# Four conditional layers in one kernel: group 0's tables beside stage 0, and the order of three pieces of work

## The reference

```
x = x + einsum('bct,bcd->bdt', x, W0[cond[b]])                 # L0: one of 16 64x64 matrices per sample
x = x + (causal_conv(x, K1) + D1 * x) * (t < len1[b])          # L1: state space kernel K1[h, 1024]
x = x + x @ W2.T + bias + scale[a] * (x @ A[a].T) @ B[a].T     # L2: over time, 1024x1024, adapter a of 8, rank 16
u = x * (t < len3[b]);  x = x + (causal_conv(u, K3) + D3 * u) * (t < len3[b])   # L3
K[h, l] = 2 Re sum_n C'[h, n] exp(dtA[h, n] * l)
```

## Time and profile before

| | us |
|---|---|
| median of 3 runs | 1615.21 (1614.43 to 1619.71) |
| the profiled execution | 1616.8, of which its span 1615.0 |
| PE busy | 1508.3 (93%) |
| DVE busy | 1251.3 (77%) |
| ACT busy | 746.6 (46%) |
| POOL busy | 573.4 (36%) |

### The profile page before, as it was taken

How to read it: one execution, slowest core, us unless ns; L and a number is a source line. 1 busy time by engine, 2 the same in 40 slices (tenths; PEclk the granted TensorE clock), 3 DMA queues, 4 the chain that set the end, 5 groups by cost and what they waited for, 6 DMA issues and landing times.

```text
span 1615.0 us, 36864 instructions
## 1 busy us (share of the span) xinstructions
PE 1508.3 (93%) x14983; PEld 1303.5 (81%) x14983; DVE 1251.3 (77%) x1525; ACT 746.6 (46%) x1083; POOL 573.4 (36%) x260
## 2 busy tenths in 40 slices
PE   7777776889999999999999999999999999999998
PEld 6677774678878787878887878788888888888887
DVE  6888876879596969697878787887878686969663
ACT  3445343435453535454545454545444454545443
POOL 2111104473333333333333434343434343434030
PEclk9898888999999999999999999999999999999999
DMA  7799995567666675757585748484848484858532
GB/s 222 254 346 380 333 373 196 126 128 186 134 170 155 155 169 137 187 126 183 128 193 118 199 113 211 99 222 90 220 97 217 90 225 100 222 103 209 110 131 67
DMA packets 455239, 287.63 MB, mean 178 GB/s; under 512 B 331512, under 2 KB 410880, under 8 KB 453056
## 3 DMA queue, kind: packets, MB, share of 16 engines
q1 hardware_dynamic: 405888, 174.57, 46.5%
q10 hardware_dynamic: 49216, 110.98, 20.2%
HBM read 161.30 MB, written 75.96 MB: 147 GB/s over the span
## 4 chain that ended last, share of the span: by engine, by line
PE 77%; DVE 11%; DMA 6%; issue 4%; ACT 2%; DVEq 0%; ACTq 0%; SPq 0%
PE ps L861 35%; PE ps L945 8%; PE ps L770 7%; PE ps L814 6%; PE ps L841 5%; DMA arena<-in_x_dram 5%; PE ps L870 5%; PE ps L958 4%; PE ps L718 3%; PE ps L780 2%; DVE arena L1790 2%; DVE gbuf L1744 1%; PE ps L654 1%; ACT arena L1297 1%; DVE arena L1635 1%
## 5 line engine op out<-in xcount | busy, mean ns | idle before, releaser
L861 PE MATMUL ps<-arena,w2t 128*128 128x256 f16 x4608 | 521.5, 273 | 0.0
L861 PEld LDWEIGHTS ps<-arena,w2t 128*128 128x128 f16 x4608 | 450.7, 98 | 55.8 <-DVE arena L1836 0.2
L588 POOL TENSOR_TENSOR arena<-arena 128x1024 f32<-128x1024 f32 x32 | 80.0, 2501 | 818.0 <-DVE arena L1797 402.6
L1840 DVE TENSOR_TENSOR arena<-arena 128x512 f16<-128x512 f32 x128 | 106.4, 831 | 125.6 <-ACT arena L1286 125.6
L1286 ACT ACTIVATE arena<-arena 128x512 f16<-128x512 f32 x128 | 80.6, 630 | 240.4 <-DVE arena L1836 239.4
L718 PE MATMUL ps<-arena 128*128 128x128 f32 x1024 | 143.3, 303 | 49.5 <-DVE arena L1635 28.2
L718 PEld LDWEIGHTS ps<-arena 128*128 128x128 f32 x1024 | 135.3, 215 | 55.1 <-DVE arena L1635 31.4
L814 PE MATMUL ps<-arena 128*128 128x512 f16 (+1 forms) x768 | 138.5, 331 | 24.2 <-DVE gbuf L1744 15.8
L1273 ACT ACTIVATE arena<-ps,biasx 128x256 f32<-128x256 f32 x256 | 105.0, 468 | 108.6 <-PE ps L861 56.9
L814 PEld LDWEIGHTS ps<-arena 128*128 128x128 f16 x768 | 72.4, 99 | 83.0 <-DVE gbuf L1744 24.2
L945 PE MATMUL ps<-arena 128*128 128x256 f16 (+1 forms) x1536 | 137.0, 246 | 0.0
(11 more groups left out here) (239 smaller groups left out, 2666.5 us busy)
## 6 DMA issues: line engine op xcount, KB each, us to landing
w2t<-w_scratch ACTq DMA_DIRECT2D x96, 512.0 KB, 4.0
arena<-in_x_dram SPq DMA_DIRECT2D x64, 512.0 KB, 8.0
out_dram<-arena SPq DMA_DIRECT2D x64, 512.0 KB, 3.4
gbuf<-x_scratch SPq DMA_DIRECT2D x120, 256.0 KB, 4.3
arena<-krow_scratch SPq DMA_DIRECT2D x32, 512.0 KB, 8.9
gbuf<-w_scratch ACTq DMA_DIRECT2D x32, 512.0 KB, 3.7
x_scratch<-arena ACTq DMA_DIRECT2D x14, 1024.0 KB, 9.4
x_scratch<-arena ACTq DMA_DIRECT2D x14, 896.0 KB, 7.6
```

Source lines behind the costliest of these rows:

```text
L861: mm = nc.tensor.matmul(ps[:, bank, n * HW:(n + 1) * HW], weight(p, n, part, k), xx[:, :, k, :], start=(fresh and n == 0 and k == 0 and q ...
L1840: tt(x3_quarter(x3l, h0, row), x3part[slot].rearrange("p (k h b) -> p k h b", k=2, h=2), x3_quarter(x3h, h0, row), ALU.subtract).then_inc( ...
```

## The change

Four edits. (1) The first row of ids has a semaphore of its own, VectorE casts it alone first, and the other two behind the one-hot and the diagonal. (2) Group 0's small tables and kernel rows are loaded ahead of the last quarter of stage 0, into weight space that is free by then; GpSimd makes group 0's u and v of L1 as soon as the last tables of buffer 0 are stored, into other tiles (`table_home`, `base_home` and `tab_home` name the new tiles for the first tables and the old ones else); ScalarE and VectorE split the bases ahead of their last copy of stage 0, one of the two last `keep_x1` copies goes to ScalarE, and `turn_g1` and `table_lo` move ahead. ScalarE's first load of a streamed weight slot also waits for g1's reversal and the finished tables, the third for the split bases. (3) In group 0 the two resident block products come ahead of the low-rank products (the 24 matmuls of L841, now `low_products()`) and wait for two x2 heads only. (4) In every body with a following group, VectorE's two past sums come two places later, behind conv rows 1 and 2.

```diff
+        v32_first = part_of(gbuf, 16, 6).rearrange("p (h n t) -> p h n t", h=HG, n=3)
+        m32_first = part_of(gbuf, 32, 4).rearrange("p (h t) -> p h t", h=HG)
+        u32_first = part_of(gbuf, 36, 4).rearrange("p (h t) -> p h t", h=HG)
+        tab_first = w2t[:, 0, 3].rearrange("p s k o -> p (s k o)").bitcast(F32)[:, 0:TAB]
+        g1n_first = w2t[:, 1:3, 3].rearrange("p q s k o -> p q (s k o)").rearrange("p q (m t) -> p q m t", t=CHUNK)
...
+        def is_first(v, g):
+            return v == 0 and isinstance(g, int) and g == 0
...
         @block.sync
-                sp.dma_start(ids[:, n, :], row.rearrange("(o b) -> o b", o=1).to_broadcast([P, B])).then_inc(ids_loaded, 16)
+                sp.dma_start(ids[:, n, :], row.rearrange("(o b) -> o b", o=1).to_broadcast([P, B])).then_inc(ids_loaded if n else ids0_loaded, 16)
             def load_g(v, g):
+                if is_first(v, g):
+                    src = bass.AP(krow_t, 0, [[1, P], [4 * KROW, 2], [KROW, 4], [1, CHUNK]])
+                    for q in range(2):
+                        sp.dma_start(to[:, q], src[:, q]).then_inc(g1_loaded, 8 * 2)
...
-            stage0(0, True)
-            with sp.Fori(1, NBLK // 2) as i:
-                stage0(i, False)
...
-            sp.wait_ge(x1_stored[0][NPART - 1], 16 * NBLK // 2)
+            stage0(0, True)
+            with sp.Fori(1, NBLK // 2 - 1) as i:
+                stage0(i, False)
             sp.wait_ge(tab_stored[0], 16)
+            sp.wait_ge(w2_turned, LOT_W + 3 * 3)
             for n in range(2):
                 load_tab(0, 0, n)
-            sp.wait_ge(s0_summed, NBLK * STEPS)
             sp.wait_ge(krow_stored, 16 + 32)
             load_g(0, 0)
+            stage0(NBLK // 2 - 1, False)
+            sp.wait_ge(x1_stored[0][NPART - 1], 16 * NBLK // 2)
             wait_u(0, 0)
             turn_u(0, 0)
...
         @block.gpsimd
             pool.wait_ge(twin_ready, 1)
-            for part in range(NPART):
-                pool.wait_ge(x1_stored[0][part], 16 * NBLK // 2)
+            pool.wait_ge(w2_turned, NLOT)
+            pool.wait_ge(w_stored, 64 * NQ)
+            pool.wait_ge(tab_stored[0], 16 * NBLK // 2)
             make_tables(0, 0)
             def body(g, more2):
                 if isinstance(g, int) and g == 0:
+                    for part in range(NPART):
+                        pool.wait_ge(x1_stored[0][part], 16 * NBLK // 2)
                     pool.wait_ge(tables_ready, NBLK)
...
         @block.tensor
             def stage2(g):
-                pe.wait_ge(x2_hi, HG * (g + 1))
-                pe.wait_ge(x2_lo, HG * (g + 1))
+                first = isinstance(g, int) and g == 0
+                pe.wait_ge(x2_hi, HG * g + 2 if first else HG * (g + 1))
+                pe.wait_ge(x2_lo, HG * g + 2 if first else HG * (g + 1))
...
+                if not first:
+                    low_products()
...
                 for p in range(2):
                     block(SUM_AT[p], p, resident(0), x2_quarter(0, 0), True, False).then_inc(s2_summed, 1)
+                if first:
+                    pe.wait_ge(x2_hi, HG * (g + 1))
+                    pe.wait_ge(x2_lo, HG * (g + 1))
+                    low_products()
...
         @block.scalar
-            copy_even(NBLK // 2 - 1, 2 * STEPS - 2)
...
+            for part in range(NPART):
+                act.wait_ge(x1_stored[0][part], 16 * NBLK // 2)
+            bases_hi(0, 0)
+            copy_even(NBLK // 2 - 1, 2 * STEPS - 2)
+            act.wait_ge(s0_even_out, NBLK * STEPS // 2)
+            nc.scalar.activation(x1f[:, :, NBLK - 2, B // 2:B], xq[:, 1, 0, 0:HG, :], ACT.Copy).then_inc(x1_kept_last, 1)
             for h in range(HG):
-                if h == 2:
-                    bases_hi(0, 0)
                 x1_split_hi(0, h)
-            table_hi(0, 0)
+                if h == 1:
+                    table_hi(0, 0)
             act.wait_ge(tab_stored[0], 16 * NBLK // 2)
+            act.wait_ge(v_lo, 1)
...
         @block.vector
-            dve.wait_ge(ids_loaded, 64)
-            nc.vector.tensor_copy(idf[:, :, :], ids[:, :, :])
-            link(nc.vector.tensor_copy(pcol, pcoli))
+            nc.vector.tensor_copy(pcol, pcoli)
+            dve.wait_ge(ids0_loaded, 16)
+            link(nc.vector.tensor_copy(idf[:, 0, :], ids[:, 0, :]))
...
+            dve.wait_ge(ids_loaded, 48)
+            nc.vector.tensor_copy(idf[:, 1:3, :], ids[:, 1:3, :])
...
             def keep_x1(i, half):
                 for k in range(2):
+                    if unit == NBLK - 1 and k == 0:
+                        continue
...
-            copy_odd(NBLK // 2 - 1, 2 * STEPS - 1)
-            keep_x1(NBLK // 2 - 1, 1)
...
+            bases_lo(0, 0)
+            copy_odd(NBLK // 2 - 1, 2 * STEPS - 1)
+            keep_x1(NBLK // 2 - 1, 1)
+            turn_g1(0)
             x1_split_lo(0, 0)
-            turn_g1(0)
             x1_split_lo(0, 1)
-            bases_lo(0, 0)
+            table_lo(0, 0)
             x1_split_lo(0, 2)
             x1_split_lo(0, 3)
-            table_lo(0, 0)
...
                     state_lo(1, g, 1)
-                    past_sum(g, 0)
                     take_conv1(g + 1, 0)
                     state_lo(1, g, 2)
-                    past_sum(g, 1)
                     take_conv1(g + 1, 1)
+                    past_sum(g, 0)
                     x2_split_lo(g + 1, 0)
                     take_conv1(g + 1, 2)
+                    past_sum(g, 1)
                     x2_split_lo(g + 1, 1)
                     take_conv1(g + 1, 3)
```

More of the change, by code:

```diff
@@ L248, in build @@
         x1_kept = sem("x1_kept")
+        x1_kept_last = sem("x1_kept_last")
+        ids0_loaded = sem("ids0_loaded")
         x1_stored = [[sem(f"x1_stored{k}{part}") for part in range(NPART)] for k in range(2)]
@@ L354, in build, with table_home, base_home, tab_home @@
         X1_ORDER = (2, 3, 0, 1)
+        def is_first(v, g):
+            return v == 0 and isinstance(g, int) and g == 0
+        def table_home(v, g):
+            return v32_first if is_first(v, g) else v32_later
+        def base_home(v, g):
+            return u32_first if is_first(v, g) else u32_ahead if made_ahead(v, g) else u32_late
+        def tab_home(v, g):
+            return tab_first if is_first(v, g) else tabs[v]
         def made_ahead(v, g):
@@ L562, in _, with left_of, right_of @@
             ptt = nc.gpsimd.tensor_tensor
-            def left_of(v, n):
-                t = tabs[v][:, n * LEFT:(n + 1) * LEFT].rearrange("p (h a) -> p h a", a=TL)
+            def left_of(tab, n):
+                t = tab[:, n * LEFT:(n + 1) * LEFT].rearrange("p (h a) -> p h a", a=TL)
                 return t[:, :, 0:TB].rearrange("p h (a o) -> p h a o", o=1).to_broadcast([P, HG, TB, TB])
-            def right_of(v, n):
+            def right_of(tab, n):
                 at0 = NLEFT * LEFT + n * HG * TB
-                t = tabs[v][:, at0:at0 + HG * TB]
+                t = tab[:, at0:at0 + HG * TB]
                 return t.rearrange("p (h o j) -> p h o j", h=HG, o=1).to_broadcast([P, HG, TB, TB])
@@ L834, in stage2, with low_products @@
             def stage2(g):
-                pe.wait_ge(x2_hi, HG * (g + 1))
-                pe.wait_ge(x2_lo, HG * (g + 1))
+                first = isinstance(g, int) and g == 0
+                pe.wait_ge(x2_hi, HG * g + 2 if first else HG * (g + 1))
+                pe.wait_ge(x2_lo, HG * g + 2 if first else HG * (g + 1))
                 products = [(0, x2h), (0, x2l), (1, x2h)]
[L839 to L843, removed]
+                def low_products():
+                    for k in range(NBLK):
+                        for q, (part, xx) in enumerate(products):
+                            mm = nc.tensor.matmul(ps[:, 7, :], at[:, part, k, :], xx[:, :, k, :],
+                                                  start=(k == 0 and q == 0), stop=(k == NBLK - 1 and q == 2))
+                    mm.then_inc(low_summed, 1)
+                if not first:
+                    low_products()
                 t_parts = [[(0, t[:, 0]), (0, t[:, 1]), (1, t[:, 0])] for t in tt_of]
@@ L1202, in x1_split_hi @@
                     act.wait_ge(x1_kept, NBLK)
+                    act.wait_ge(x1_kept_last, 1)
                 else:
@@ L1303, in _ @@
                     act.wait_ge(w_stored, 64 * NQ)
+                    act.wait_ge(v_made, 2)
+                    act.wait_ge(g1_turned, 1)
+                if j == 2:
+                    act.wait_ge(u_lo, 1)
                 load_w(j)
@@ L1694, in _ @@
                 stage0(i, False, i == NBLK // 2 - 1)
-            copy_odd(NBLK // 2 - 1, 2 * STEPS - 1)
-            keep_x1(NBLK // 2 - 1, 1)
             def turn_g1(g):
-                dve.wait_ge(g1_loaded, 16 * (g + 1))
+                dve.wait_ge(g1_loaded, 16 * (g + 2))
                 at_least(dve, c1_summed, HG * g)
                 if isinstance(g, int) and g == 0:
+                    dve.wait_ge(g1_loaded, 32)
```

(6 more changed lines are left out.)

29 lines of the change are left out of this document (16 added, 13 removed).

## The result

The changed kernel took 1608.88 us (median of 5 runs, 1607.45 to 1612.2), the kernel before 1618.78 beside it: ratio 0.9951, 95% interval 0.9935 to 0.9966. A second series with the changed kernel gave 1606.77 against 1616.79, ratio 0.9944 (0.9925 to 0.9963). So it is some 8 to 10 us faster, 0.5 to 0.6%, where 22.1 were forecast, and 1608.88 lies above the range of 1586 to 1607. The profiled execution took 1609.9 us, its span 1608.1.

What follows compares the result with a forecast made beforehand. Limits: DMA in stage 0, a VectorE, ScalarE and GpSimd chain in the hand-over, TensorE in fifteen groups. 0.2 + 6.9 + 2.7 + 12.3 = 22.1 us off 1616.8 gave 1594.7, from the median 1593.1; it said 1594, range 1586 to 1607.

Steps and rivals of the forecast that it cites:

- Start, 0.2: Kernel start: casting one row of ids first makes the ready signal earlier; 0.2 us gained, bounds 0 and 0.5.
- Hand-over, 6.9: From stage 0 to group 0's first far product: earlier tables and states bring it to 269.9; 6.9 us gained, bounds 2 and 9.
- its sign of 253 to 257: Hand-over: the first near product was to begin at 253 to 257 us; after 259 the prediction is wrong.
- Resident product first, 2.7: Group 0: resident blocks ahead of the low-rank products spare TensorE's idle stretch and shorten VectorE's chain; 2.7 us, bounds 0 and 6.4.
- the 4.0 us wait before group 1's states: TensorE at the end of group 0's mixing: gated by VectorE's chain, this wait would grow to 10 us.
- Convolution rows ahead of the past's sum, 12.3: Steady groups: TensorE's wait for conv rows shrinks; 0.9 us 13 times and 0.6 for group 0's pair, 12.3 us.
- the first: Rival: the hand-over's gain is lost in a longer wait before group 1's states; 1602 us, chance 0.16.
- The second: Rival: the steady gain becomes a wait for conv row 3 in the last convolution, 0.2 a group kept; 1604 us, chance 0.10.
- The third: Rival: four hand-over VectorE instructions take 3.37 us each beside GpSimd, past sums leave 0.2 a group; 1611 us, chance 0.08.

Runs made afterwards that it cites:

- after_again: The changed kernel measured once more, nothing altered: 1606.77 us against 1616.79 for the kernel before, ratio 0.9944.
- low_first: The changed kernel with group 0's low products ahead of the resident block again: 1609.78 us, ratio 0.9952 to the kernel before.
- pool_later: The changed kernel, with GpSimd starting a group's second set of tables only after two low parts of the next x: 1592.97 us, ratio 0.9856.
- read_only: The kernel before with ScalarE's early read of the sum bank alone, VectorE's order unchanged: ratio 0.9999, period 82.93 us.

## Why the prediction was wrong

By its own steps:

- **Start, 0.2**: right; TensorE's first wait ended at 10.57 and not 10.76. Whatever of it lasts is part of the 7.0 us below.
- **Hand-over, 6.9**: right within 1.8 us. The mean over the executions is 7.0, the first far product at 269.94 where 269.9 was said; agreement to a tenth is chance. Its parts differ: 8.3 against the 8.7 between the last x tiles and that product, and 1.3 against the 1.8 of a longer stage 0. In the first profiled execution it showed as 4.1, and the first near product (258.14) lay outside its sign of 253 to 257, because that execution had one of the latest x tiles (247.05); in `after_again` it began at 254.53. bases_lo, beside GpSimd, took the 3.27 us that the step feared (in the nine executions 1.2 to 3.3, where 2.5 was said), and the step still held.
- **Resident product first, 2.7**: wrong, 0.0. What it counted on happened: VectorE's idle 3.12 us before L1827 became 0.93, and L1885 began 6.3 us earlier where the hand-over alone gave 4.1. But that chain did not set the end of the group: TensorE's lead was lost in other waits and in the clock behind one of them, as `low_first` shows. And the 4.0 us wait before group 1's states, said to grow to 10, stayed 4.0.
- **Convolution rows ahead of the past's sum, 12.3**: this is the step that failed. It measured 1.0 at group 1 (102.97 us from the first far product to group 1's low products, for 103.98), 13 x 0.184 = 2.4, and -0.6 at the last group: 2.8. Its arithmetic on the side it looked at was sound: conv row 3 was awaited for only 0.17 us at L945's place, VectorE's idle 1 us was there, and 81.77 us was reached as soon as the other limit was gone (82.0 was said). What it left out is TensorE's other obligations in the group. It asked who is late next at the last convolution, the low products and the states, and not at the reads of the sum banks in stage 2, where ScalarE's order left 0.4 us. In its place the runs showed TensorE waiting 0.82 us a group for such a read, which costs 0.98 of the 1.16 us that the new order could give. So the term was 13 x 0.18 and not 13 x 0.9.

The sum of measured parts is 7.0 + 0.0 + 2.8 = 9.8 us, and the medians differ by 9.9 and 10.0, closer than the error of the first part lets one expect. With ScalarE's reads moved, the kernel takes 1594.88 us: the forecast of 1594 was near the time of a kernel with both limits removed, partly by luck, as the 2.7 us for group 0 never came and each steady group gave 1.16 us and not 0.9.

Of the rivals, the first is out: the hand-over's gain was kept, and the wait before group 1's states is 4.0 us in the kernel before and in the changed one. The second had the right shape and nearly the right size (0.2 a group kept, 3 us), but named conv row 3 as the new wait; its 1604 came out too low mainly by group 0's 2.7. By the time alone the third, 1611, is as near. The third's mechanism, VectorE held up beside GpSimd, cost little in the hand-over, where it was priced for four instructions (two of them, keep_x1 and turn_g1, have one input, and turn_g1 took 0.68 us behind GpSimd's last instruction); it is what made the read late in the steady groups, as `pool_later` shows. The rule of the Trainium skill, "SBUF — State Buffer", section "Who interferes with whom", bears on it, and the trace agrees: the split started at 976.36 beside a GpSimd instruction that ran from 976.11 to 978.22 and ended at 979.31, 1.09 us behind it, where alone it takes 1.23.

## What to carry to other kernels

When a wait of w us is removed from a tight loop, every other wait of the same engine in that loop moves w earlier: list for each one the slack now (its releaser's end against the engine's start, less the 0.14 us that passed here between the two where the engine did wait), also where the profile shows no wait at all, and credit only the smallest. Here that was under 0.3 us, and 0.18 came of the 1.13. A releaser's own length says little where its engine works through a fixed order; a 0.8 us read was late through the 2 us of splits ahead of it, and the remedy was to move it ahead of them. And where one execution scatters by more than a step is worth, compare intervals within the trace (33.9 against 25.6 us) before blaming or crediting the step.

## What the runs showed of the hardware

- Stage 0 is bound by DMA (a share of 0.99), and its last x tiles come anywhere between 239.5 and 247.1 us over all executions with a trace, 241.0 to 247.1 over nine with the same code in that stage; this accounts for most of the scatter of the total (`low_first` 1603.0 us with 241.0, the first execution after the change 1609.9 with 247.1; the kernel before 1616.8 with 243.1, `read_only`, as fast, 1613.1 with 239.5).
- TensorE's clock after short idle times. In the changed kernel the granted clock was 1.00 from 307 to 311 us, in which it worked for 1.5 us of 4, and 0.64 from 311 to 315, after the wait of 2.50 us had ended, so the 24 matmuls behind that wait took 4.22 us and not 2.78. The wait thus cost 2.5 + 1.4 us. Behind the waits of 0.8 us in the steady groups and of 1.25 us at 279.98 the matmuls kept their pace (2.78 us for 24, 5.40 for 48).

```profile
307.00:311.00 4.00, 1.50 (x39) 1.19 (x37) 4.00 (x3) 3.25 (x5) 3.92 (x2) 1.00 0.41 134
311.00:315.00 4.00, 4.00 (x24) 2.97 (x25) 4.00 (x3) 1.84 (x5) 3.92 (x3) 0.64 0.13 21
```

(Windows of the changed kernel: stretch in us, length, busy time of TensorE, weight load, VectorE, ScalarE, GpSimd, then granted clock, DMA share, GB/s.)
